# Packing the two halves of V into one stationary tile, a second copy of the output weights, and an interleaved ending, in a two-layer kernel on one core

## The reference

```python
x = x + s0 * silu(moe(xn))                 # layer 0
xn = layernorm(x)
q, k, v = heads(xn @ Wq.T), heads(xn @ Wk.T), heads(xn @ Wv.T)   # 32, 8, 8 heads of 64
q, k = rope(q), rope(k)
p = softmax(mask(q @ k.T / 8))             # causal, 512 x 512; k and v shared by 4 query heads
s = (p @ v) @ Wo.T
g = silu((sign(layernorm(xn) * gamma + beta) @ sign(W - mean(W)).T + bias) * alpha)
out = x + s * g
```

## Time and profile before

| | us |
|---|---|
| median of 3 runs | 755.84 (753.89 to 756.01) |
| the profiled execution's own time | 756.22 |
| its span, first to last instruction | 754.4 |
| PE, DVE, ACT, POOL busy | 711.2, 489.7, 416.7, 384.5 |
| mean granted TensorE clock | 0.984 of full speed |

### The profile page before, as it was taken

How to read it: one execution, slowest core, us unless ns; L and a number is a source line. 1 busy time by engine, 2 the same in 40 slices (tenths; PEclk the granted TensorE clock), 3 DMA queues, 4 the chain that set the end, 5 groups by cost and what they waited for, 6 DMA issues and landing times.

```text
span 754.4 us, 13451 instructions
## 1 busy us (share of the span) xinstructions
PE 711.2 (94%) x4576; PEld 622.9 (83%) x4576; DVE 489.7 (65%) x1036; ACT 416.7 (55%) x1043; POOL 384.5 (51%) x437
## 2 busy tenths in 40 slices
PE   2999999999999999699989999999999999999995
PEld 2887998988998888587778888888888888888884
DVE  7583555434323335898867777877777777777764
ACT  4436343242341342547667677767766677767662
POOL 1412442432323222137565777777876778677450
PEclk9899999999999999899999999999999999999998
DMA  8175877787878646145432332233222422132001
GB/s 293 41 227 179 284 247 236 230 254 250 252 239 246 196 140 170 33 115 183 115 106 53 89 81 53 65 77 82 65 57 72 92 67 63 46 85 57 2 1 56
DMA packets 103828, 98.06 MB, mean 130 GB/s; under 512 B 50576, under 2 KB 74064, under 8 KB 103632
## 3 DMA queue, kind: packets, MB, share of 16 engines
q1 hardware_dynamic: 101648, 91.43, 41.4%
q0 software_dynamic: 2112, 5.77, 2.3%
HBM read 69.24 MB, written 11.14 MB: 107 GB/s over the span
## 4 chain that ended last, share of the span: by engine, by line
PE 68%; DVE 11%; POOL 8%; ACT 8%; issue 4%; DMA 1%; SPq 0%; DVEq 0%; ACTq 0%; POOLq 0%
PE bank L1670 14%; PE bank L1530 8%; PE bank L1531 8%; PE bank L1532 8%; PE bank L1704 8%; PE bank L1526 8%; POOL prob L1488 4%; ACT prob L1294 3%; PE bank L1810 3%; PE bank L1811 3%; DVE nmax L1042 2%; ACT p_hi L1301 2%; POOL q_lo L1500 2%; DVE o_lo L1055 1%; PE bank L1813 1%
## 5 line engine op out<-in xcount | busy, mean ns | idle before, releaser
L1488 POOL TENSOR_TENSOR prob<-prob,rinv 128x128 f32<-128x128 f32 (+3 forms) x256 | 178.9, 731 | 106.4 <-DVE rinv L1047 106.4
L1294 ACT ACTIVATE prob<-bank,nmax 128x512 f32<-128x512 f32 (+3 forms) x256 | 133.4, 529 | 51.7 <-DVE nmax L1042 45.7
L1051 DVE TENSOR_TENSOR p_lo<-bank,p_hi 128x512 fp32r<-128x512 f32 x160 | 110.0, 687 | 48.8 <-ACT p_hi L1301 47.8
L1301 ACT ACTIVATE p_hi<-bank 128x512 fp32r<-128x512 f32 x160 | 96.3, 602 | 70.5 <-PE bank L1526 70.4
L1670 PEld LDWEIGHTS bank<-xgT,wm 128*128 128x128 f32 x920 | 108.7, 192 | 4.5 <-issue 2.9
L1670 PE MATMUL bank<-xgT,wm 128*128 128x128 f32 x920 | 111.3, 275 | 0.5 <-ACT xgT L1210 0.5
L1526 PE MATMUL bank<-cst,prob 128*128 128x128 f32 x640 | 97.4, 275 | 2.0 <-ACT prob L1294 1.2
L1042 DVE TENSOR_REDUCE nmax<-bank 128x1 f32<-128x512 f32 (+2 forms) x192 | 91.1, 502 | 6.2 <-PE bank L1813 5.5
L1530 PE MATMUL bank<-p_hi,v_lo 128*128 128x128 f32 (+3 forms) x256 | 92.8, 362 | 0.3 <-DVE p_lo L1051 0.3
L1810 PE MATMUL bank<-kT,qT 128*128 128x512 f32 (+3 forms) x256 | 81.5, 324 | 4.4 <-ACT prob L1294 4.3
L1459 POOL DMA_INDIRECT y_rows<-y_row,to_row x21 | 22.8, 1084 | 118.2 <-DVE y_row L911 92.5
(11 more groups left out here) (309 smaller groups left out, 1529.3 us busy)
## 6 DMA issues: line engine op xcount, KB each, us to landing
wm<-in_w_moe SPq DMA_DIRECT2D x23, 1280.0 KB
wm<-in_w_moe SPq DMA_DIRECT2D x23, 640.0 KB
qT<-q_hi SPq DMA_DIRECT2D x124, 64.0 KB, 2.0
qT<-q_lo SPq DMA_DIRECT2D x124, 64.0 KB, 2.0
k_exp<-k_rows SPq DMA_DIRECT2D x56, 64.0 KB, 2.0
wtl<-in_w_moe_tail SPq DMA_DIRECT2D x46, 64.0 KB
y_rows<-gate SPq DMA_DIRECT2D x1, 2048.0 KB, 14.1
wq_raw<-in_w_qkv SPq DMA_DIRECT2D x32, 64.0 KB, 2.5
```

The costliest lines, as they stand in the source:

```text
L1051: TT(p_lo[:, b_, :], bank[2 + b_ % 2][:, :], p_hi[:, b_, :].bitcast(F32), ALU.subtract).then_inc(plo_done, 1)
L1294: ins = actv(prob[:, i % 2, h, POFF[j]:POFF[j] + (j + 1) * P], bk[:, at:at + (j + 1) * P], ACT.Exp, bias=nmax[:, i % 2, h, j:j + 1], accum ...
L1301: actv(p_hi[:, b_, :], bank[2 + b_ % 2][:, :], ACT.Copy).then_inc(phi_done, 1)
L1488: ins = GT(seg, seg, rinv[:, i % 2, k, j:j + 1].to_broadcast([P, (j + 1) * P]), ALU.mult)
```

## The change

- v in one tile. `v_parts` (P x 8 x 192) holds upper, lower, upper. Head 0's stationary tile is the columns 0 to 127 (upper | lower), head 1's 64 to 191 (lower | upper). One pass with `p_lo` and one with `p_hi` take the place of three. Head 0 has bank 4, head 1 bank 5, for every pair; in the 64 rows that are not the head's own the bank holds the product with v's lower part.
- `TURNED` is reordered (head 0 complete after step 2, head 1 after step 4); the block (head 1, key tile 0) is written in two halves of 256 columns.
- O becomes O and R for each head: ACT copies 64 rows (`o_hi`, zeroed once by POOL's memset), and DVE's R, priority 3.2 and so behind T, takes `o_hi` off the head's own rows with one scalar_tensor_tensor over 128 rows, with a per-row factor -1 or 0 (`minus`, written by four memsets in DVE's start-up). `o_rest0` has both batches, `o_rest1` one.
- W uses the weights doubled over both row halves (`wo_twice`, filled from `wo_hi` by 4 new DMAs a group, `double_wo`) and has 8 matmuls instead of 6.
- N's priority is 2.6: on DVE it stands behind the maximum and ahead of T.
- ACT's copy of v's upper part writes both upper thirds (128x512 instead of 128x256).
- G is spread over the steps 15 to 18, one in each.
- The ending: Z one step apart and from step 0 of the tail, ordered by batch; the gate's multiplication (M), the transposes back (B) and the addition to x (X) of batch 0 stand in the tail's lists among batch 1's last steps; batch 1 is transposed by output half as each is multiplied; three stores (512, 256, 256 KB) instead of two.

```diff
-TURNED = [[(0, 0, 0)], [(0, 1, 0), (0, 3, 3 * P)], [(1, 0, 0)], [(1, 1, 0), (1, 3, 3 * P)], [(0, 2, 0), (1, 2, 2 * P)]]
+TURNED = [[(0, 0, 0)], [(0, 1, 0), (0, 3, 3 * P)], [(0, 2, 0), (1, 2, 2 * P)], [(1, 0, 0)], [(1, 1, 0), (1, 3, 3 * P)]]
+VALUED = (2, 4)
+VALUED_BY = {(1, 0): [(0, 2 * P), (2 * P, HALF)]}
...
-            own += [(5 * r + HEADS_AT[h], 5, "N", r, h)]
-        own += [(5 * r + 4 + LAG + TO_V + 1, 1, "O", r, 0)]
+            own += [(5 * r + HEADS_AT[h], 2.6, "N", r, h)]
+        own += [(5 * r + VALUED[h] + LAG + TO_V + 1, p, op, r, h) for h in range(2) for p, op in ((1, "O"), (3.2, "R"))]
...
-            ready += [(16 + k // 2, 8.4, "G", k, 0)]
+            ready += [(15 + k, 8.4, "G", k, 0)]
...
-    ends = [(4 + 2 * n, 8.6, "Z", n, 0) for n in range(KC * BATCH)]
+    ends = [(n, 8.6, "Z", n, 0) for n in range(KC * BATCH)]
+    ends += [(4 + m, 9, "M", m, 0) for m in range(KC)] + [(10 + m, 9, "M", m, 1) for m in range(KC)]
+    ends += [(6 + n, 9, "B", n, m) for n in range(2) for m in range(KC)] + [(11 + m, 9.1, "B", n, m) for m in range(KC) for n in (2, 3)]
+    ends += [(8 + n, 9.2, "X", n, 0) for n in range(2)] + [(13, 9.2, "X", n, 0) for n in (2, 3)]
...
+            def double_wo(g):
+                sp.wait_ge(wohi_done, g + 1)
+                for h in range(2):
+                    for to in range(2):
+                        sp.dma_start(wo_twice[to * HD:(to + 1) * HD, :, h, :].bitcast(F32),
+                                     wo_hi[h * HD:(h + 1) * HD, :, :].bitcast(F32)).then_inc(twice_in, 16)
...
-                        dve.wait_ge(ohi_done, q + 1)
-                        TT(o_lo[:, b, m, :], bank[4 + m][:, :], o_hi[:, b, m, :].bitcast(F32), ALU.subtract).then_inc(olo_done, 1)
+                        dve.wait_ge(ohi_done, 2 * q + k + 1)
+                        if q == 0:
+                            dve.wait_ge(o_zero, 1)
+                        if k == 1 and m == 0 and q > 0:
+                            dve.wait_ge(wo_full, g * (BATCH * KC) + 2 * b + 1)
+                        to = o_rest1[:, m, :] if k else o_rest0[:, b, m, :]
+                        STT(out=to, in0=o_hi[:, b, m, :].bitcast(F32), scalar=minus[:, k:k + 1], in1=bank[4 + k][:, :],
+                            op0=ALU.mult, op1=ALU.add).then_inc(olo_done, 1)
...
-                        actv(o_hi[:, b, m, :], bank[4 + m][:, :], ACT.Copy).then_inc(ohi_done, 1)
+                        if k == 1:
+                            act.wait_ge(olo_done, 2 * q + 1)
+                        hs = slice(k * HD, (k + 1) * HD)
+                        actv(o_hi[hs, b, m, :], bank[4 + k][hs, :], ACT.Copy).then_inc(ohi_done, 1)
...
                     elif op == "A":
                         pe.wait_ge(plo_done, u + 3)
                         if k == 0:
-                            pe.wait_ge(olo_done, q + 1)
                             if i % 2 == 0:
                                 pe.wait_ge(vlo_done, g * 2 + (b + 1))
+                            if q > 0:
+                                pe.wait_ge(olo_done, 2 * q - 1)
+                        if k == VALUED[0] and q > 0:
+                            pe.wait_ge(olo_done, 2 * q)
...
-                            n = (TB - j) * P
-                            dst = bank[4 + i % 2][:, j * P:j * P + n]
-                            vs = slice(HD, 3 * HD) if h == 0 else slice(0, 2 * HD)
-                            last = k == 4 and h == 1
-                            ins = split3(dst, v_hi[:, b * TB + j, vs], v_lo[:, b * TB + j, vs], p_hi[:, b_, at:at + n],
-                                         p_lo[:, b_, at:at + n], k == 0, last)
+                            vs = v_parts[:, b * TB + j, h * HD:(h + 2) * HD]
+                            for p, first, end in ((p_lo, True, False), (p_hi, False, True)):
+                                for x, y in VALUED_BY.get((h, j), [(j * P, HALF)]):
+                                    ins = mm(bank[4 + h][:, x:y], vs, p[:, b_, at + x - j * P:at + y - j * P],
+                                             start=first and (h, j) in ((0, 0), (1, 2)), stop=end and (h, j) in ((0, 2), (1, 3)))
...
                         for c in range(2):
-                            ins = split3(bank[6 + m][:, :], wo_hi[:, c, m * P:(m + 1) * P], wo_lo[:, c, m * P:(m + 1) * P],
-                                         o_hi[:, b, c, :], o_lo[:, b, c, :], c == 0, c == 1)
+                            mm(dst, wo_twice[:, c, 0, ms], o_rest0[:, b, c, :], start=c == 0, stop=False)
+                            mm(dst, wo_twice[:, c, 1, ms], o_rest1[:, c, :], start=False, stop=False)
+                            mm(dst, wo_lo[:, c, ms], o_hi[:, b, c, :], start=False, stop=False)
+                            ins = mm(dst, wo_hi[:, c, ms], o_hi[:, b, c, :], start=False, stop=c == 1)
```

More of the change, by code:

```diff
@@ L201, in layered_kernel @@
         ab = sb("ab", [P, KC], F32)
+        minus = sb("minus", [P, 2], F32)
         low = (nc.sbuf_base + 31) // 32 * 32
@@ L381, in layered_kernel @@
         o_hi = attn("o_hi", [P, 2, 2, HALF], F32R)
-        o_lo = attn("o_lo", [P, 2, 2, HALF], F32R)
+        o_rest0 = attn("o_rest0", [P, 2, 2, HALF], F32R)
+        o_rest1 = attn("o_rest1", [P, 2, HALF], F32R)
         def k_mix(r, b):
@@ L632, in _ @@
             load_v(1, 1)
+            double_wo(0)
             load_wo(1)
@@ L643, in group @@
                 load_v(g + 1, 1)
+                double_wo(g)
                 load_wo(g + 1)
@@ L649, in _ @@
             move_q(KVH - 1, 1)
-            for b in range(BATCH):
-                sp.wait_ge(x_ready, NT // 2 + (b + 1) * TB // 2)
-                ts = slice(b * TB, (b + 1) * TB)
+            double_wo(KVH - 1)
+            for lo, hi in ((0, TB), (TB, TB + 2), (TB + 2, NT)):
+                sp.wait_ge(x_ready, NT // 2 + hi // 2)
+                ts = slice(lo, hi)
                 sp.dma_start(out.rearrange("(t p) c -> p t c", p=P)[:, ts, :], x_tok[:, ts, :]).then_inc(out_done, 16)
-            sp.wait_ge(out_done, BATCH * 16)
+            sp.wait_ge(out_done, 3 * 16)
         @block.vector
@@ L708, in _ @@
             then(vec.memset(chosen[:, NT, :], 0.0))
+            for h in range(2):
+                then(vec.memset(minus[h * HD:(h + 1) * HD, h:h + 1], -1.0))
+                then(vec.memset(minus[(1 - h) * HD:(2 - h) * HD, h:h + 1], 0.0))
             vec.memset(ptl[0:TAIL, :, :], 0.0).then_inc(pad_zero, 1)
@@ L1106, in _ @@
             attend(KVH, schedule("tail"))
[L1107 to L1116, removed]
-                TT(xt2, xt2, bank[n][:, :].rearrange("p (t c) -> p t c", c=C), ALU.add).then_inc(x_ready, 1)
         @block.scalar
@@ L1272, in upper_q, with upper_v @@
                 actv(q_hi[:, :, :], q_mix[:, :, 0, :], ACT.Copy).then_inc(qhi_done, 1)
+            def upper_v(ts, src):
+                return actv(v_parts[:, ts, :].rearrange("p t (a d) -> p t a d", a=3)[:, :, 0:3:2, :],
+                            src.unsqueeze(2).to_broadcast([P, TB, 2, HD]), ACT.Copy).then_inc(vhi_done, 1)
             def upper_k(now, i):
@@ L1333, in attend @@
                             act.wait_ge(av_done, now * STEPS + (10 * i - 6))
-                        actv(v_hi[:, ts, HD:2 * HD], v_all[:, ts, 0:HD] if now == 0 else v_exp[:, ts, :], ACT.Copy).then_inc(vhi_done, 1)
+                        upper_v(ts, v_all[:, ts, 0:HD] if now == 0 else v_exp[:, ts, :])
                     elif op == "F":
@@ L1461, in _ @@
             gp_.wait_ge(row_full, NJ)
-            for v in (v_hi, v_lo):
-                for z in (0, 2):
-                    pool.memset(v[:, :, z * HD:(z + 1) * HD].bitcast(F32), 0.0).then_inc(vpad_ready, 1)
+            pool.memset(o_hi[:, :, :, :].bitcast(F32), 0.0).then_inc(o_zero, 1)
             def split_wq(g):
@@ L1866, in attend @@
                         held[i % 2] = (sign_ready, i + 1)
+                    elif op == "B":
+                        b = i // 2
+                        pe.wait_ge(sg_ready, KC * b + k + 1)
+                        if i < 2:
+                            pe.wait_ge(g1_ready, KC * BATCH)
+                        for t in range(2):
+                            ins = tr(bank[i][:, (t * KC + k) * P:(t * KC + k + 1) * P],
+                                     sT[:, k, (2 * i + t) * P:(2 * i + t + 1) * P])
+                        if k == KC - 1:
+                            ins.then_inc(back_full, 1)
                     elif op == "Z":
-                        m, s = i // 2, i % 2
+                        m, s = i % 2, i // 2
                         if i > 1:
@@ L1911, in _ @@
             attend(KVH, schedule("tail"), [(w_added[m], (KVH - 1) * BATCH) for m in range(KC)])
-            for n in range(NT // 2):
-                pe.wait_ge(sg_ready, KC * (n // (TB // 2) + 1))
-                for j in range(2 * KC):
-                    t, m = 2 * n + j // KC, j % KC
-                    ins = tr(bank[n][:, j * P:(j + 1) * P], sT[:, m, t * P:(t + 1) * P])
```

(1 more changed line is left out.)

39 lines of the change are left out of this document (25 added, 14 removed).

## The result

The changed kernel takes 748.01 us (median of four runs, 746.42 to 748.34), the kernel before 755.0 beside it: ratio 0.9906, 95% interval 0.9889 to 0.9922. It is faster by 7 us, not by the forecast 20; the range held it, and the time is the second rival's 747. The profiled span went from 754.4 to 746.5.

The account below looks back on a forecast made before the run. PE was taken as only partly the bound: full in loaded stretches, while the chain maximum, exponential, scores ties bare ones. Half groups 16, G 3 and ending 1 sum to 20 us gained: 736 us, range 721 to 750.

Parts of the forecast that it names:

- The ending: After the last group: earlier multiplications, transposes and additions and a shorter last store gain net 1 us (-2 to 3).
- second rival: The element-wise chain takes all of the bare stretch, R eating what the lost `o_hi` wait gives: 747 us, chance 0.18.
- loaded stretch: Half group's five steps with two W and two Q besides S, T, A: 0.65 us gained, 0.34 PE, 0.3 POOL.
- third rival: Slower: banks 4 and 5 are single, so A waits for R of the head before: 765 us, chance 0.09.
- fourth rival: The clock falls in the bare stretches, once a half group, taking all back: 756 us, chance 0.03.
- Fourteen half groups from group 1 to 7: 16 us: Main term: each half group gains 1.15 us, fourteen of them 16 us (4 to 28).
- Bare stretch: Half group's five steps with only S, T and A on PE: 0.5 us gained of PE's 1.26.
- Group 7: Group without Q, to its last S: gains 2.3 us, at the same price per half group.
- Group 1: First of the groups priced by half groups: gains 2.3 us.
- Nothing is exposed: The four new DMAs a group land in 2.0 us, six steps before W reads them: no cost.
- G with group 0: G spread over steps in group 0 removes PE's wait and the clock dip: 3 us gained (1 to 6).
- The first: Rival: PE is the bound throughout, so all its saved work counts: 35 us gained, 721 us, chance 0.15.

Follow-up runs that it names:

- experiment 1: Kernel before, with A leaving out the product of v's lower part and the upper probabilities (two passes instead of three): 741.5 us, ratio 0.9821.
- 9: Changed kernel without the two matmuls of `wo_twice` and `o_rest1` in each W (6 instead of 8): 733.28 us, ratio 0.9711.
- experiment 2: Changed kernel with N back behind T on DVE (priority 5): 757.49 us, ratio 1.0030.
- experiment 4: Changed kernel with the old ending: multiplications, transposes and additions behind the last W, three stores kept: 750.29 us, ratio 0.9942.
- 8: Changed kernel with R over 256 of its 512 columns, the rest left at zero: 744.46 us, ratio 0.9864.
- experiment 7: Changed kernel with only R a step later, behind the maximum, and O where it was: 746.64 us, ratio 0.9878.
- experiment 6: Changed kernel with O behind the exponential of its step and R a step later, ahead of T; run twice: 743.34 and 743.16 us.
- experiment 3: Changed kernel with G in pairs as before (two in step 16, two in step 17): 747.88 us, ratio 0.9899.
- experiment 11: Kernel of experiment 6 with Q and its ropes one step earlier, q's additions, copy and split in place: 744.95 us, ratio 0.9868.
- the last version: Kernel of experiment 6 with the middle groups' W in bare steps, a second `o_rest1`, and POOL's split of output weights at step 21: 737.21 us, ratio 0.9775.
- 13: Kernel before with N earlier, G spread, O behind the exponential and the `o_lo` subtraction a step later; v, W, ending as before: 741.39 us, ratio 0.9822.
- experiment 12: Kernel of experiment 6 with the middle groups' W in bare steps and a second `o_rest1`: 745.8 us; with POOL's weight split at step 21: 737.21 us.
- experiment 10: Changed kernel with all of q's work, Q and ropes included, one step earlier: 793.53 us, ratio 1.0518.

## Why the prediction was wrong in size

**Right:** PE saves 1.26 us of A a pair and pays 0.92 for W a half group, and both are seen in full where PE is the bound (experiment 1's loaded stretch of 13.40, where 14.67 was, and 9). R's 0.737 us (0.744 taken) and `o_hi` of 64 rows at 0.589, as long as one of 128 (0.62) are right. The wait for `o_hi` is gone, the banks of one head each cost nothing in the middle groups (third rival), the clock is 1.00 from 342 to 740 (fourth rival), the dip at 382 is gone. N's early place is "what lets PE run faster there at all", in one of the two loaded stretches: experiment 2. The ending gave 1.1 by the trace from its first T on and 2.0 by experiment 4, where 1 was forecast, but the steps ahead of it gave 1 back.

**The step that failed** is "Fourteen half groups from group 1 to 7: 16 us". The trace has 6.6 (the table's -6.9, +0.1 and +0.2, where 16 stood). Its parts:

- *Bare stretch*, "0.5 us gained of 1.26": 0.21 came. The fourth S was right. For the fifth the prediction saw R "ahead of the next maximum on DVE" and let it gain nothing; it lost 0.1 (7.42, before 7.3). The sixth, "I count the sixth S at 9.1", comes 2.0 us behind the fifth, and by the chain that is PE's own S, T and A; the prediction had allowed 1.8 (7.3 to 9.1). What sets the fifth is DVE's list with R in it: experiments 8 and 7 take half of R or all of it out of that place and shorten the stretch by 0.28 and 0.55 us; 6 moves O too and gives 0.39. The prediction set "neither is full" from a group's sums (DVE 40.5, and 40.01 came), right after it had said that such sums mislead. In the bare stretch itself DVE is 89% busy and runs 8 us without a gap. O's place on ACT, ahead of an exponential, looks like a second hold, but neither the chain nor experiment 7 shows it as one in a middle group; O moved alone wasn't run.
- *Loaded stretch*, "PE's 0.34, plus about 0.3 that T stood for POOL: 0.65": 0.62 in the stretch of the earlier trace rows, 0.32 in the other of the group. PE's part came in both. The wait for POOL stood only in the stretch that the prediction had read (POOL 13.08 of 14.97, which it called full); in the other POOL had 11.52 of 14.67. A half group gained 0.69 on the mean of groups 2 to 6, not 1.15.
- *Group 7*, 2.3: 0.2 was lost. It has three Q fewer, and PE isn't full even in its loaded stretches (11.69 of 12.10). These gained 0.16 and 0.19, but its bare ones grew, from 9.72 to 10.05 and from 7.95 to 8.05 (the second counted to the last S); experiments 7 and 6 find 1.1 and 1.6 us in the group by the places of R and of O. The forecast used one price for all 14 halves, though the earlier trace rows had shown group 7 to be bound otherwise, and the text said so.
- *Group 1*, 2.3: 0.1 was lost. "Nothing is exposed" was wrong for the first group's copies of `wo_twice`: PE stands 0.86 us for them, and the step is 1.1 longer than the same step half a group on. In experiment 3, without this wait, group 1 gains 1.1. The prediction had counted six steps between `wo_hi` and W, but not the store that stands ahead of the copies in SP's queue in group 0.

**The other term:** G with group 0 was sized 3, and 0.9 came. Spreading G is worth 2.1 in group 0 by experiment 3 and 0.9 with what group 1 gives back; by the trace the last five steps of group 0 gained 1.4, and step 13 lost 1.0 (PE idle 2.3 us before 368.55, where it was idle 1.1 before). The idle and the low clock were read rightly; that ACT, busy all through the low stretch, covers part of PE's lateness is argued, not shown.

**The rivals.** The second rival is nearest, in time (747 against 748.0) and in mechanism: R in the bare stretch eats what the lost wait gives. It is not quite that, since 0.21 did come. That its 747 was so near is partly luck: it has all 14 loaded stretches at 0.34 and G with the ending at 4, while the loaded stretches of groups 2 to 6 gained 0.47 on the mean, groups 1 and 7 nothing, and G with the ending about 1. The first falls with experiment 1.

**Open:** the first part of the kernel varies by some 2 us between runs (layer 1's first masked scores at 332.0 to 334.3), and groups 0 and 1 by over 1 (102.6 and 104.0 us in the two runs of experiment 6), which hides effects of 1 us in the totals. Step 13 of group 0, the loss in experiment 11 and the unequal groups of the last version aren't explained.

## What to carry to other kernels

An engine that is 98% busy over a group need not be the bound of each stretch: take a third of its work away in one experiment and see which stretches move. Where they don't, write out the in-order lists of the other engines between two events of the chain; an instruction that stands ahead of the chain's own can cost its time, waited for or not, and moving two of them (experiment 6, and 13 without the packing) gave as much as or more than 25.6 us less matmul work. A price read in one stretch holds for that stretch: read its sister too, and the first and the last group, where the queues hold other work (the copies of `wo_twice` were exposed only in the first). Work added to the engine that binds in one stretch is best put where it idles, and what feeds it must not end up ahead of another chain (the two versions of experiment 12).

## What the hardware showed unexpectedly

- ACT's copy of 64 rows x 512 columns out of a bank takes 0.589 us, that of 128 rows (`p_hi`, 77 of them in the same 180 us) 0.596: half the rows save nothing. Splitting an ACT copy by rows costs a whole copy more.
- How long PE was idle does not by itself tell whether the granted clock falls. In the changed kernel it stayed at 1.00 (2.4 GHz) from 342 to 740, with ten waits for exponentials in 180 us, the longest 1.2, and with single gaps of 2.3 us before 368.55 and 2.46 before 720.02. The gaps of 1.9 us in experiment 2, 2.2 in 7, 2.47 before the change and 2.88 in experiment 3 were followed by some 3 us or more at 0.50 (1.2 GHz), and so were nine of the twelve gaps of 1.8 us in experiment 10. The Trainium skill ("TensorE: Matmul & The Clock Gate", section "A second HAM failure mode: psum-queue depth-cycling") warns that short idles can bring the clock down; the middle groups of the changed kernel do not show it, those of experiment 10 do.
- What the low level costs depends on the stretch. With PE full, 3.4 us of it made a loaded stretch of 14.32 us into one of 15.89 (experiment 10). In experiment 3 an idle of 2.88 us and 6.8 us at the low level together made group 0 only 2.1 longer, with ACT busy 5.94 of 6.00 us.
